# A hybrid of causal, gated and biased attention on one core: a fixed place in the cycle for each step, first and last layers given memory side by side, value products in quarters

## The reference

```python
x = x + attn_a(layernorm(x))   # causal, rotated q and k, 16 heads of 16
x = x + ffn(layernorm(x))      # gated: see below
x = x + attn_b(layernorm(x))   # 16 heads of 64, scores + rel_bias[j - i + ...]
x = x + ffn(layernorm(x))
```

## Time and profile before

| | |
|---|---|
| median of 3 runs | 2450.35 us (2449.46 to 2453.07) |
| profiled execution | 2451.99 us, span 2450.3 us |
| TensorE busy | 2231.9 us, 91% of the span |
| TensorE weight loads | 1335.0 us, 54% |
| VectorE, ScalarE, GpSimd busy | 53%, 46%, 21% |
| mean granted TensorE clock | 0.986 |
| read from HBM, written | 91.49 MB, 4.19 MB |

### The profile page before, as it was taken

How to read it: one execution, slowest core, us unless ns; L and a number is a source line. 1 busy time by engine, 2 the same in 40 slices (tenths; PEclk the granted TensorE clock), 3 DMA queues, 4 the chain that set the end, 5 groups by cost and what they waited for, 6 DMA issues and landing times.

```text
span 2450.3 us, 38728 instructions
## 1 busy us (share of the span) xinstructions
PE 2231.9 (91%) x15600; PEld 1335.0 (54%) x15616; DVE 1308.7 (53%) x3536; ACT 1131.7 (46%) x2033; POOL 524.9 (21%) x755
## 2 busy tenths in 40 slices
PE   5779899898999989999999999999999999998996
PEld 3444556554565535655466554665546654565564
DVE  4446544656536556456555565554663656546334
ACT  2224555445435554355452555425543455435552
POOL 2101312122302312022311123111321112301220
PEclk9889999999999999999999999999999999999998
DMA  3001011111001200112011110112010111001100
GB/s 116 1 1 35 31 44 65 44 65 40 23 24 49 71 28 22 38 50 67 16 38 35 55 49 16 44 35 70 29 37 23 50 55 44 23 22 50 67 22 9
DMA packets 28913, 98.16 MB, mean 40 GB/s; under 512 B 2752, under 2 KB 11328, under 8 KB 28608
## 3 DMA queue, kind: packets, MB, share of 16 engines
q1 hardware_dynamic: 28736, 95.70, 11.4%
HBM read 91.49 MB, written 4.19 MB: 39 GB/s over the span
## 4 chain that ended last, share of the span: by engine, by line
PE 75%; DVE 17%; ACT 4%; issue 2%; DMA 1%; POOL 0%; SPq 0%
PE ps L584 21%; PE ps L958 9%; PE ps L1201 9%; PE ps L1187 8%; PE ps L1194 8%; DVE mcol L896 4%; DVE probs L915 4%; DVE mcol L828 4%; PE ps L1026 3%; PE ps L1002 3%; PE ps L1143 3%; PE ps L1130 2%; PE ps L1040 2%; ACT PTc L698 2%; PE ps L1111 1%
## 5 line engine op out<-in xcount | busy, mean ns | idle before, releaser
L736 ACT ACTIVATE probs<-probs,peak 128x512 f32<-128x512 f32 x512 | 364.9, 713 | 395.0 <-DVE peak L921 395.0
L667 POOL TENSOR_SCALAR probs<-probs,rtotal 128x512 f32<-128x512 f32 x512 | 343.3, 692 | 819.3 <-DVE rtotal L925 819.3
L915 DVE CUSTOM_DVE_ANT_0 probs<-ps,band 128x512 f32<-128x512 f32 x512 | 332.7, 687 | 180.9 <-PE ps L1187 180.2
L743 ACT ACTIVATE PT<-ps 128x1024 f32<-128x1024 f32 x256 | 254.1, 1018 | 87.4 <-PE ps L1194 86.8
L1187 PE MATMUL ps<-KT,QT 64*128 64x512 f32 x1024 | 278.6, 635 | 8.4 <-DVE mcol L896 4.2
L1194 PEld LDWEIGHTS ps<-ident,probs 128*128 128x128 f32 x2048 | 224.9, 141 | 89.1 <-issue 83.7
L1194 PE MATMUL ps<-ident,probs 128*128 128x128 f32 x2048 | 264.8, 276 | 3.9 <-DVE mcol L896 2.3
L828 DVE TENSOR_REDUCE mcol<-ps 128x2 f32<-128x1024 f32 (+3 forms) x256 | 194.6, 817 | 97.3 <-PE ps L1006 96.4
L584 PE MATMUL ps<-xnT,wb 128*128 128x512 f32 x512 | 234.9, 599 | 3.0 <-DMA wb<-in_w_b 2.6
L1201 PE MATMUL ps<-PT,Vb 128*64 128x512 f32 x1024 | 233.8, 598 | 1.2 <-ACT PT L743 1.2
L698 ACT ACTIVATE PTc<-ps 128x768 f32<-128x768 f32 (+1 forms) x192 | 157.0, 882 | 89.8 <-PE ps L1026 89.8
(11 more groups left out here) (125 smaller groups left out, 3007.8 us busy)
## 6 DMA issues: line engine op xcount, KB each, us to landing
band<-in_band SPq DMA_DIRECT2D x64, 896.0 KB, 4.6
wb<-in_w_b SPq DMA_DIRECT2D x64, 384.0 KB, 3.0
x<-in_x SPq DMA_DIRECT2D x8, 512.0 KB, 3.8
out<-x SPq DMA_DIRECT2D x16, 256.0 KB, 2.2
wob<-in_wo_b SPq DMA_DIRECT2D x1, 1024.0 KB, 7.1
wqk<-in_wqk_a SPq DMA_DIRECT2D x1, 512.0 KB, 4.5
wva<-in_wv_a SPq DMA_DIRECT2D x1, 256.0 KB, 4.1
woa<-in_wo_a SPq DMA_DIRECT2D x1, 256.0 KB, 4.2
```

The lines of the kernel that those rows point to most:

```text
L667: last = g.tensor_scalar(unit, unit, rtotal[:, r % 8, e:e + 1], 1.0, ALU.mult, ALU.mult)
L736: last = a.activation(unit, unit, ACT.Exp, bias=peak[:, r % 8, e:e + 1], accum_out=total[:, r % 8, e:e + 1])
L743: a.activation(PT[:, k % 2, :, :, tile_of(q)], bank(now).rearrange("p e (k n) -> p e k n", k=NT), ACT.Copy).then_inc(act_read, 1)
L915: last = v.tensor_tensor_reduce(out=probs[:, r % ROWS_HELD, e, :], in0=bank(now)[:, e, :], in1=band[:, k % 2, e, lo:lo + T], scale=1.0, sc ...
```

## The change

It has five parts.

- The first block is gone. SP issues the loads at the head of the main block, x in two halves with a semaphore each, sequence 1's x ahead of the output weights; each user waits for its own load. GpSimd writes the small constants; `mcol` and `Vx` are written by VectorE, and a second pair of them by GpSimd behind the first rstd.
- Causal and gated layers get a second set of tiles, laid over the memory of the biased layer (QT2 up to OTb). `place_of` gives it to sequence 1's causal layer and to sequence 7's last gated layer. `whole()` lets sequence 1's causal layer start at once, and biased layer 0 follows it; the last gated layer no longer follows the one of sequence 6.
- `in_order` takes the ready step with the smallest number in a table, `PLACE`, plus 2898 (`CYCLE`) for each sequence. Rows of the table are for the first layers (`first0`, `first1`, `first`), for all cycles between (`cycle`, `cycle3`) and for the last (`last2`, `last1`, `last`); a step of n and q has its own number. `WORK` has new durations; they and the engines' times are used only to choose banks. Two-bank units may start at odd banks. `EARLY` is gone.
- `b_val` becomes four steps (four matmuls each) and each `b_y` two; the parts share a bank and one evacuation. `f_rank`'s second unit becomes a step `f_spread`. `b_row`'s two products get a bank unit each, `o` and `o2`, with a semaphore count each.
- Some waits are added for orders that are now possible, such as `f_p2` of group 1 for `f_spread`'s evacuation and `c_y` for both `c_ot`.

```diff
-    "b_row": [("o", "dve", 2)], "b_tr": [("o", "act", 2)], "b_val": [("o", "dve", 1)], "b_y": [("o", "dve", 1)],
+    "b_row": [("o", "dve", 1), ("o2", "dve", 1)], "b_tr": [("o", "act", 2)], "b_val": [("o", "dve", 1)], "b_y": [("o", "dve", 1)],
+PARTS = {"c_val": 3, "b_val": 4, "b_y": 2}
...
+CYCLE = 2898
+PLACE = {
+    ("cycle", "b_row"): [1089, 974, 1186, 1173, 1239, 1208, 1545, 993, 1620, 1226, 1446, 1283, 1601, 1722, 1499,
+        1737, 1612, 1884, 2008, 1862, 2284, 2598, 2259, 2872, 2973, 3006, 3063, 2489, 3201, 3288, 3372, 3446],
+    ("cycle", "b_tr"): [1350, 1432, 1569, 1677, 1671, 1041, 1730, 1260, 1747, 1960, 1817, 1989, 2279, 2282, 2188,
+        2517, 2764, 2786, 2990, 2978, 2801, 3029, 2936, 3216, 3386, 3198, 3434, 3589, 3698, 3501, 3318, 2925],
+    ("cycle", "b_val"): [1774, 1474, 1332, 1825, 2000, 1973, 1793, 2193, 2720, 2441, 2659, 2749, 3003, 2448, 3009,
+        2968, 3177, 2804, 3258, 2669, 3455, 3531, 3153, 3614, 3753, 3597, 2843, 3751, 3324, 3761, 3627, 3666],
+    ("cycle", "c_y"): [58, 57],
+    ("cycle", "f_ln"): [76],
+    ("cycle", "f_row"): [107],
+    ("cycle", "f_m"): [309, 334, 467, 451],
+    ("cycle", "f_p1"): [220, 242, 422, 408],
+    ("cycle", "f_p2"): [367, 362, 487, 74],
...
+    ("last", "b_val"): [22642, 22401, 22503, 22955, 23030, 21839, 22453, 22624, 22728, 22636, 22610, 22134, 23284,
...
+    ("last2", "f_y"): [22158, 21589],
...
+def place_of(s, l):
+    return int((s, l) in ((1, 0), (B - 1, 3)))
...
-    entered = add(causal_steps(0), [], [])
-    side = entered = add(ffn_steps(0, 1), entered, [])
+    causal = [add(causal_steps(s), [], []) for s in range(2)]
+    entered = [add(ffn_steps(0, 1), causal[0], [])]
+    side = add(ffn_steps(1, 1), causal[1], entered[0])
+    entered.append(side)
     for s in range(B):
-        biased = add(biased_steps(s, s - 1 if s else None), entered, [])
+        layer = biased_steps(s, s - 1 if s else None)
+        if s == 0:
+            layer = [(x, a, b + causal[1] * (x.kind == "b_k" and x.n == 0)) for x, a, b in layer]
+        biased = add(layer, entered[s], [])
...
-    add(ffn_steps(B - 1, 3), left, side)
+    add(ffn_steps(B - 1, 3), left, [])
...
+def turn(x):
+    row, cycle = stage(x)
+    return PLACE[row, x.kind][x.n * SEVERAL.get(x.kind, 1) + x.q] + CYCLE * cycle
...
+        x = min((x for x in ready if not (xn_held and x.kind in ("c_ln", "f_ln", "b_ln"))), key=lambda x: (turn(x), number[x]))
...
+                        if kind == "b_val":
+                            if q == 0:
+                                read(now, Step("b_tr", s, l, n, NT - 1))
+                                read(now, Step("b_v", s, l, n))
+                                room(now)
+                            for e in range(2):
+                                last = te.matmul(o[half(e), :], Vb[:, k % 3, q, half(e)], PT[:, k % 2, e, q, :],
+                                                 start=(q == 0), stop=(q == NT - 1))
```

More of the change, by code:

```diff
@@ L27 @@
 ROWS_HELD = 6
+CONSTS = 9
 SBUF_FROM, SBUF_TO = 16512, 229376
 Step = namedtuple("Step", "kind s l n q", defaults=(0, 0))
-Unit = namedtuple("Unit", "bank banks reader no freed")
+Unit = namedtuple("Unit", "banks reader no freed")
+Causal = namedtuple("Causal", "Qz K1 PTc partner xnTc qk strips OTa on mcol Vx rsums")
+Gated = namedtuple("Gated", "Qzf K1f PTf pick logit_junk gate_row above tie stripsf onf OTf spread_t xgT of mcolf Vxf rsums z "
+                   "gate rank")
 UNITS = {
@@ L93 @@
[L93 to L104, removed]
@@ L136 @@
[L136 to L141, removed]
+CHANGE, PE_OUT, SIGNAL, HAND_OVER = 0.1, 0.2, 0.07, 0.06
@@ L313, in in_order @@
+        emptied = {"act": [], "dve": []}
+        ends = []
+        for i, op in enumerate(work[x]):
+            engine, us = op[:2]
+            if i:
+                j = op[2] if len(op) > 2 else i - 1
+                before = work[x][j][0]
+                t = ends[j] + (0 if before == engine else PE_OUT if before == "pe" else SIGNAL)
+            t = max(t, free[engine]) + us
             free[engine] = t
-            if i and engine != "pool":
+            ends.append(t)
+            if i and engine in emptied:
@@ L315, in in_order @@
                 emptied[engine].append(t)
[L316 to L326 removed]
+        done[x] = max(ends)
@@ L963, in _ @@
                         kind, s, l, n, q = now
+                        m = memory(now)
                         if kind not in UNITS:
@@ L1184, in _ @@
                             read(now, Step("b_k", s, l, n))
-                            room(now)
-                            for e in range(2):
-                                last = te.matmul(o[:, e, :], QT2[half(e), k % 2, tile_of(q)], KT2[half(e), k % 2, :],
-                                                 start=True, stop=True)
+                            for e, name in enumerate(("o", "o2")):
+                                room(now, name)
+                                full(te.matmul(bank(now, name), QT2[half(e), k % 2, tile_of(q)], KT2[half(e), k % 2, :],
+                                               start=True, stop=True), now, name)
+                            continue
                         if kind == "b_tr":
@@ L1195, in _ @@
                         if kind == "b_val":
-                            read(now, Step("b_tr", s, l, n, NT - 1))
-                            read(now, Step("b_v", s, l, n))
-                            room(now)
-                            for t in range(NT):
-                                for e in range(2):
-                                    last = te.matmul(o[half(e), :], Vb[:, k % 3, t, half(e)], PT[:, k % 2, e, t, :],
-                                                     start=(t == 0), stop=(t == NT - 1))
```

817 lines of the change are left out of this document (514 added, 303 removed), and 3 rows, old and new, of the table WORK.

## The result

The changed kernel takes 2349.29 us (median of 4 runs, 2345.19 to 2349.65) beside 2450.15 for the kernel before: a ratio of 0.9582, 95% interval 0.9566 to 0.9599. The forecast was 2351.

A forecast was written before the change was run, and what follows sets the result against it. TensorE was taken to bound the kernel, with 218.4 us idle to win. Start 44, next stretch 3, middle 51 and tail 1 sum to 99 us, giving a 2351 us median; likeliest range 2312 to 2390, to 2425 with A.

The forecast's parts named there:

- The block at the start: Kernel start: without the first block each user waits for its own load, TensorE begins at 7.7 us; 5.5 us gained.
- Causal layer 1 beside causal layer 0: First 180 us: sequence 1's causal layer fills TensorE's holes, leaving 15 us; gain 33 us, ends 20 and 42.
- the next stretch: The 180 to 300 us stretch: 3 of its 10.1 us of TensorE idle time gained.
- the clock term: First 180 us: 8 us taken as lost to low clock, 6 of it recovered once the holes close.
- The last two gated layers: Tail: the table leaves them apart, the gate wait stays, 1 us gained; truly together, up to 20 us more.
- The cycle: Middle, 6.95 cycles: the table's fixed places let half the short waits go; 7.4 us gained per cycle, 51 in all.
- The Qzf waits: Sign in the cycle: TensorE's waits for maxima added to Qzf fall from 35 occurrences to a handful.
- The price of a change of shape: TensorE in the cycle: each change of tile shape costs 0.12 us; split quarters cost 1.2 us a cycle.
- Rival D: TensorE's busy time shrinks too: about 150 shape changes a cycle halved, 64 us on top, 2287 us; chance 0.05.
- A (the start alone): Only the start gains and the cycle's short waits change place: 2404 us, from 2390 to 2425; chance 0.20.
- C (nothing to measure): The cycle grows by 6 to 7 us, so nothing is measured; chance 0.03.
- B (fixed order stalls): The table leaves chains uncovered in the cycle, making the kernel slower; 2514 us with five such chains; chance 0.09.

The follow-up runs named there:

- two pairs of runs: Start in series, then side by side: under the planner of before with the new steps, 2477.86 and 2446.70 us; under the table, 2413.60 us and the changed kernel's 2349.29.
- the joined form with the banks kept: The changed kernel with each pair's four value quarters directly behind one another, every unit keeping its bank of the changed kernel: 2379.74 us.
- the series start with the table: The changed kernel with sequence 1's causal layer put back beside biased sequence 0, the cycle keeping the table's places: 2413.60 us, ratio 0.9843.
- the joined quarters with banks of their own: The changed kernel with each pair's four value quarters directly behind one another and banks chosen anew: 2440.72 us.
- the run without weight waits: The changed kernel with each pair's q and k biased weights fetched as soon as b_q is done, the v part behind b_v: 2319.14 us, ratio 0.9457.

## Why the prediction was right, point by point

The time came out 2 us from the forecast, and that closeness is in part luck. The mechanism was right: the holes at the start were filled, and the cycle lost idle time. But the terms add up to some 102 us less idle time (5.5 + 33 + 3 + 1, and 6.95 cycles at 9.3 less 0.7) and a busy time 2 us longer (6.95 x 1.2, less 6 for the clock); measured were 70.6 us less idle time and a busy time 32.0 us shorter. The holes of the start and the idle time of the cycle were both put too high, and the fall of the busy time, which nothing in the forecast but 6 us of clock stood for, made up for it. The mean granted clock went from 0.986 to 0.992, about 15 us of the span as an estimate; the rest of the fall is not explained in full.

- **The block at the start** (5.5 us): first TensorE work at 7.13, forecast 7.7. Right in size where it arises; with the wait for the six loads put back, 5.0 us show at sequence 1's xnT and are not visible at the end.
- **Causal layer 1 beside causal layer 0** (33 us of holes, 6 of clock, 3 in the next stretch): with 1.42 cycles at 7.4 the terms give 57.5 us to sequence 2's xnT, measured 60.1. The split was not as forecast. Over the first 300 us idle time fell by 33.6 us (70.9 to 37.3), where the block, the holes and the next stretch had 41.5: 32.75 us stay idle in the first 180, 7.1 of them ahead of the first work, so 25.6 us of holes are left and not 15. Busy time up to sequence 2's xnT fell by 19.5; less 1.42 cycles at 2.7 and 16 matmuls fewer, some 13 us by this estimate, are the start's, where the clock term had 6. The two pairs of runs set its price between 31 and 64 us; 39 lies between, and neither pair is a clean one. (VectorE's share of the causal layer sums to 49.7 us in the table of durations, not 48; nothing changes by it.) The clock was to be near 1.00 in the first 180 us and is 0.96. The busy time's share lost to it went from 14.3 us (119.20 x 0.12) to 5.9 (147.25 x 0.04), so 8.4 us came back where the term had 6. Most of what the column still shows as lost (15.71 busy us at 0.74, so 4.1) lies from 100 to 120 us, below.
- **The last gated layers stay apart** (1 us): the 5.7 us gate wait is there. From sequence 7's xnT to the end 7.5 us went, where the terms give 4.9 (0.53 of a cycle at 7.4, and 1). From the transposes of the last gate row to the end it takes 53.7 us and not 55.2, so 1.5 less where 1 was forecast; the rest lies beside biased layer 7. Right in kind; putting them together, for which I had held up to 20 us possible, cost 5 in the one order tried.
- **The cycle** (7.4 us each): measured 7.0 to 7.1. The two halves of the term were both off, against each other. Idle time fell by 4.5 us a cycle, not 9.3, mostly because the weight wait took 3.5 of them (23.5 us over 6.8 cycles); without it the fall is 8.2 (18.6 to 10.4). The Qzf waits, which were to become a handful, are 13. I had read the distances of rows, gates and maxima, and left out the one queue with a transfer in it, SP's: a step that was moved closer to the next user of its buffer. Without that wait a cycle gains 11.7 us. Busy time was to rise by 1.2 us through changes of tile shape and fell by 2.7 (2.4 between cycles whose clock reads 1.00, 276.00 and 273.63); why is open but for the part that goes with waits, below. Counted from the order, such changes are 135 a cycle before and 133 after, so no rise was due; the splits took the place of changes that were there, which the term allowed for only in part.
- **The price of a change of shape** (0.12 us): the joined form with the banks kept has 124 changes a cycle, 9 fewer, and its busy time is 274.3 us in a cycle whose clock reads 1.00, where the change has 273.6: not 1.1 less but 0.7 more. It has more waits as well, and busy time moves with them, so a small price could be hidden. The rule of the Trainium skill (TensorEngine Tiling (Array Packing), "Key Properties"), that changing the tiling mode drains TensorE, finds no visible price here. No run altered the number of changes by itself, so how much each costs stays open. Rival D's 150 changes a cycle came from dividing 18.6 us by 0.12; the order has 135.
- **The rivals.** A (the start alone) is excluded by cycles of 288 us, and by the series start with the table, at 2413.6 us still 37 faster than before. C (nothing to measure) needed cycles that grow by 6 to 7 us, and falls with it. B (fixed order stalls) is not what happened, but the joined quarters with banks of their own show how near it lay: 91 of the 101 us of gain are gone, 61 of them by the banks. The waits of the transposes for probs that would have shown the forecast wrong did not appear (one of 0.3 us, as before). D's mark, a busy time that falls, did appear (2.7 us a cycle), not by its mechanism. In the run without weight waits the busy time fell a further 1.1 us a cycle (0.8 at equal clock) with not one TensorE instruction moved, so part of what the rows call busy goes with the waits.

## What to carry to other kernels

When an order written out by hand replaces a planner, list for each moved step not only what it computes for, but which buffer it frees and which queue refills it: here a transfer of some 3 us had 1.5 us of other work to hide behind, and fetching the parts as each is done gave 30 us on top of the change's 101. Keep the choice of banks fixed when only the order is meant to vary; in one and the same order one choice of banks cost 61 us, twice what the moved steps were, and another with as many differences cost nothing. Products cut into quarters pay where TensorE would otherwise wait for a chain on another engine: three of seven places carried 17 of 30 us beside VectorE's gate and output rows, and one more covered 7.4 us of waits for GpSimd.

## What the runs showed of the hardware

The granted clock fell in the middle of the start, where TensorE's longest wait between 80 and 120 us was 2.38 us. Two stretches of 20 us of the change:

```profile
80.00:100.00 20.00, 18.38 (x216) 10.66 (x213) 8.61 (x16) 12.82 (x19) 6.21 (x9) 1.00 0.01 2
100.00:120.00 20.00, 15.71 (x117) 8.79 (x115) 18.65 (x41) 0.20 (x1) 1.40 (x2) 0.74 0.00 1
```

and TensorE's timeline there:

```profile
104.04 1.14 PE L1308 MATMUL ps<-K,Qz 32*128 32x512 f32 x8
105.11 0.40 PE L1312 MATMUL ps<-later,identb 128*128 128x128 bf16 x4
107.90 2.09 PE L1308 MATMUL ps<-K,Qz 32*128 32x512 f32 x8 [2.38 <-DVE mcol L1131]
```

The same eight products take 1.14 us and, behind a wait of 2.38 us for VectorE (busy 18.65 of 20 us there), 2.09: near the ratio of the two clock levels, 2.4 and 1.2 GHz. The first projection shows the same: four products in 3.78 us at 12.60, behind the waits of the start, and four of the same shape in 1.88 at 30.24, though the clock column of the first 20 us says 1.00. So the column need not show every slow stretch; the duration of a repeated shape does. Which waits bring the clock down and which don't, these runs don't tell apart.
